# A recommender's attention kernel: the bias of the attended history goes through the first layer once, and the end of the program is put in another order

## The reference

```python
cand = candidate_features @ Wi + bi                  # 512 x 64
hist = history_features @ Wi + bi                    # 512 x 200 x 64
hidden = relu((cand @ Wq)[:, None, :] + hist @ Wk)
scores = where(mask, hidden @ Wv, -1e9)
attn = softmax(scores, axis=1)
interest = einsum('bs,bse->be', attn, hist)
avg = sum(hist * mask, axis=1) / lens
x = concatenate([interest, cand, avg], axis=1)       # 512 x 192
x = relu(bn(x @ W1 + b1)); x = relu(bn(x @ W2 + b2)); x = relu(bn(x @ W3 + b3))
return sigmoid(x @ Wo + bo)[:, 0]
```

## Time and profile before

| what | us |
|---|---|
| median of three runs | 212.09 (210.8 to 212.43) |
| the profiled execution's own time | 211.71 |
| its span, first to last instruction | 209.7 |
| PE busy in the span | 200.9 |
| DVE busy in the span | 176.8 |
| ACT busy in the span | 103.5 |
| POOL busy in the span | 62.6 |

### The profile page before, as it was taken

How to read it: one execution, slowest core, us unless ns; L and a number is a source line. 1 busy time by engine, 2 the same in 40 slices (tenths; PEclk the granted TensorE clock), 3 DMA queues, 4 the chain that set the end, 5 groups by cost and what they waited for, 6 DMA issues and landing times.

```text
span 209.7 us, 6308 instructions
## 1 busy us (share of the span) xinstructions
PE 200.9 (96%) x2126; PEld 83.6 (40%) x2126; DVE 176.8 (84%) x1086; ACT 103.5 (49%) x302; POOL 62.6 (30%) x112
## 2 busy tenths in 40 slices
PE   7999999999999999999999999999999999997793
PEld 3422434343434434343434343343444343433422
DVE  1458578989989898989899898989898998998890
ACT  2145355545465553555453655535554536556523
POOL 7903330606051321406060513224060605131000
PEclk9999999999999999999999999999999999999985
DMA  6999999797979797987969797978879793000000
GB/s 201 398 426 416 412 419 391 245 328 249 323 245 322 237 320 266 309 307 269 321 242 300 268 323 237 316 262 317 303 253 326 238 318 130 0 0 5 3 0 0
DMA packets 10225, 53.72 MB, mean 256 GB/s; under 512 B 1105, under 2 KB 2001, under 8 KB 10194
## 3 DMA queue, kind: packets, MB, share of 16 engines
q1 hardware_dynamic: 9906, 52.95, 70.7%
q10 hardware_dynamic: 288, 0.37, 0.6%
HBM read 53.32 MB, written 0.00 MB: 254 GB/s over the span
## 4 chain that ended last, share of the span: by engine, by line
PE 87%; DVE 8%; ACT 2%; issue 2%; DVEq 0%; ACTq 0%
PE hist_ps L396 42%; PE key_ps L411 24%; PE score_ps L422 10%; PE attn_ps L441 5%; DVE scratch L552 3%; DVE kept L539 3%; PE score_ps L366 2%; PE score_ps L473 1%; PE score_ps L465 1%; ACT hidden L306 1%; ACT x L326 1%; PE score_ps L468 0%; PE hist_ps L411 0%; ACT result L334 0%; DVE attended L552 0%
## 5 line engine op out<-in xcount | busy, mean ns | idle before, releaser
L306 ACT ACTIVATE hidden<-key_ps,query 128x200 f32<-128x200 f32 x252 | 86.8, 427 | 54.3 <-PE key_ps L411 54.3
L396 PE MATMUL hist_ps<-history,params 128*64 128x400 f32 x512 | 100.3, 512 | 0.0
L539 DVE SCALAR_TENSOR_TENSOR kept<-item,lens,hist_ps 128x200 f32<-128x200 f32 x256 | 92.7, 419 | 7.2 <-PE hist_ps L396 7.2
L552 DVE CUSTOM_DVE_ANT_0 scratch<-attn_ps,kept 128x200 f32<-128x200 f32 x240 | 73.3, 363 | 9.2 <-PE attn_ps L441 9.2
L411 PE MATMUL key_ps<-kept,params 64*64 64x400 f32 x504 | 57.0, 521 | 0.9 <-ACT hidden L306 0.4
L396 PEld LDWEIGHTS hist_ps<-history,params 128*64 128x64 f32 x512 | 31.2, 136 | 37.1 <-issue 28.4
L259 POOL TENSOR_SCALAR attn<-weights,inv_sum 128x200 f32<-128x200 f32 x15 | 6.5, 435 | 112.6 <-DVE inv_sum L567 112.6
L411 PEld LDWEIGHTS key_ps<-kept,params 64*64 64x64 f32 x504 | 13.6, 131 | 35.9 <-issue 26.7
L422 PE MATMUL score_ps<-hidden,wv_rows 128*32 128x200 f32 x512 | 25.3, 336 | 1.2 <-ACT hidden L306 1.2
L441 PEld LDWEIGHTS attn_ps<-parts,spread 64*64 64x64 bf16 x480 | 15.7, 107 | 24.5 <-issue 19.0
L314 ACT ACTIVATE weights<-scores,neg_max 128x200 f32<-128x200 f32 x16 | 7.4, 462 | 35.5 <-DVE neg_max L561 35.5
(11 more groups left out here) (69 smaller groups left out, 59.0 us busy)
## 6 DMA issues: line engine op xcount, KB each, us to landing
history<-history_dram SPq DMA_DIRECT2D x63, 800.0 KB, 5.0
history<-history_dram SPq DMA_DIRECT2D x2, 400.0 KB, 4.7
candT<-candidates_dram SPq DMA_DIRECT2D x1, 256.0 KB, 5.5
params<-parameters_dram SPq DMA_DIRECT2D x1, 248.5 KB, 12.1
params<-parameters_dram ACTq DMA_DIRECT2D x1, 226.5 KB, 2.4
lens_raw<-lengths_dram ACTq DMA_DIRECT2D x1, 136.0 KB, 3.8
probability<-result SPq DMA_DIRECT2D x1, 2.0 KB
```

The source lines that it names most:

```text
L306: act.activation(hidden[:, g % HID_SLOTS, v, :], banks[:, v, at * SEQ:(at + 1) * SEQ], ACT.Relu, bias=query[:, 2 * g + v:2 * g + v + 1]).t ...
L396: product = pe.matmul(hist_ps[64 * h:64 * h + 64, g % 2, 0:QCOLS], param("wi"), history[:, slot, h, 2 * at:2 * at + 2, :].rearrange("f p s ...
L539: dve.scalar_tensor_tensor(out=kept[:, g % KEPT_SLOTS, u, :], in0=item[:, :], scalar=pair_len[:, col:col + 1], in1=hist_ps[:, g % 2, u * S ...
L552: dve.tensor_tensor_reduce(scratch[:, at, v, :], banks[:, at, v * SEQ:(v + 1) * SEQ], kept[:, q % KEPT_SLOTS, v, :], 1.0, 0.0, ALU.mult, A ...
```

## The change

The addition of bi to the attended sums goes: a matmul of one column puts bi through the first layer's weights once, ACT copies the result to `fold_bias`, POOL adds it to the first layer's shift, and stage 1 of the network reads `attended`. PE does that matmul in unit 5, behind the projections; ACT the copy behind `relu(5)`; POOL waits for the copy within its batch norm chain. Fewer matmuls on zeros are issued: 4 for 6, 2 for 4, 2 for 6. The network's parts become 228 and 28 pairs, so that `mean(0)` comes one unit earlier in the loop (unit 59). At the end `mean(1)` stands before the attended sums of unit 57, the fourth sum of unit 59 stands behind the first instruction of the last split, ACT does stage 1 of part 0 before it loads the sigmoid's table, and PE and ACT do stages 2 to 4 of part 0 earlier.

```diff
+FOLD_AT = 5
-MORE_WARMUPS = 6
-GAP_WARMUPS = 4
-TAIL_WARMUPS = 6
+MORE_WARMUPS = 4
+GAP_WARMUPS = 2
+TAIL_WARMUPS = 2
-PART_UNITS = UNITS - 6
+PART_UNITS = FREE_AT
...
@@ gpsimd
             pool.wait_ge(bn_steps, 3)
+
+            pool.wait_ge(fold_ready, 1)
+            pool.tensor_tensor(bn_shift[:, 0:1], bn_shift[:, 0:1], fold_bias[:, :], ALU.add).then_inc(bn_steps, 1)
             pool.tensor_tensor(bn_scale[:, :], bn_scale[:, :], bn_power[:, :], ALU.pow).then_inc(bn_steps, 1)
-            pool.wait_ge(bn_steps, 4)
+            pool.wait_ge(bn_steps, 5)
...
@@ scalar, the loop over units and the end
                 relu(unit)
+                if unit == FOLD_AT:
+                    act.wait_ge(fold_product, 1)
+                    act.activation(fold_bias[:, :], attn_ps[:, 1, 0:1], ACT.Copy).then_inc(fold_ready, 1)
             exponent(LAST)
+            mlp_stage(0, 1)
             act.activation(table_loader[:, :], param("bo", slice(0, 1)), ACT.Sigmoid)
-            for stage in range(1, 4):
-                mlp_stage(0, stage)
+            mlp_stage(0, 2)
+            mlp_stage(0, 3)
+            mlp_stage(0, 4)
             mlp_stage(1, 1)
             mlp_stage(1, 2)
-            mlp_stage(0, 4)
             mlp_stage(1, 3)
             mlp_stage(1, 4)
@@ tensor
                 if stage == 1:
-                    pe.wait_ge(interest_ready, n + 1)
+                    pe.wait_ge(attn_summed, pairs.stop)
...
-                        product = pe.matmul(z1[:, h, pairs], w1[rows, 0, :], interest[rows, pairs],
+                        product = pe.matmul(z1[:, h, pairs], w1[rows, 0, :], attended[rows, pairs],
...
+                if unit == FOLD_AT:
+                    pe.wait_ge(late_landed, 16)
+                    pe.wait_ge(bias_ready, 1)
+                    pe.matmul(attn_ps[:, 1, 0:1], w1[0:EMB, 0, :], param("bi", slice(0, EMB)),
+                              start=True, stop=True).then_inc(fold_product, 1)
...
                         pe.wait_ge(query_ready, 1)
+                        pe.wait_ge(fold_ready, 1)
                     spread_attn(unit - DELAY)
...
             for _ in range(TAIL_WARMUPS):
                 keep_busy((LAST + 1) % 2)
+            mlp_stage(0, 2)
             spread_attn(first + 3)
             spread_attn(first + 4)
-            mlp_stage(0, 2)
+            mlp_stage(0, 3)
             spread_attn(first + 5)
-            mlp_stage(0, 3)
             spread_attn(first + 6)
+            mlp_stage(0, 4)
             mlp_stage(1, 0)
-            mlp_stage(0, 4)
@@ vector
-            def store_interest(n):
...
             first = UNITS - DELAY
+            mean(1)
             attended_sum(first)
-            store_interest(0)
-            mean(1)
             attended_sum(first + 1)
             maximum(LAST)
-            attended_sum(first + 2)
+            attended_sum(first + 2, (0, 1, 2))
             invert(LAST)
...
             dve.tensor_scalar(part_a[:, :], weights[:, bank, :], inverse, param("keep1"),
                               ALU.mult, ALU.mult).then_inc(split_steps, 1)
+            attended_sum(first + 2, (3,))
...
             for unit in range(first + 3, UNITS):
                 attended_sum(unit)
-            store_interest(1)
```

More of the change, by code:

```diff
@@ L110, in build @@
         attended = sb("attended", [128, HALF])
-        interest = sb("interest", [128, HALF])
+        fold_bias = sb("fold_bias", [128, 1])
         average = sb("average", [128, HALF])
@@ L180, in build @@
         average_ready = sem("average_ready")
-        interest_ready = sem("interest_ready")
+        fold_product = sem("fold_product")
+        fold_ready = sem("fold_ready")
         z1_ready = sem("z1_ready")
@@ L282, in _ @@
             pool.wait_ge(bn_steps, 3)
+            pool.wait_ge(fold_ready, 1)
+            pool.tensor_tensor(bn_shift[:, 0:1], bn_shift[:, 0:1], fold_bias[:, :], ALU.add).then_inc(bn_steps, 1)
             pool.tensor_tensor(bn_scale[:, :], bn_scale[:, :], bn_power[:, :], ALU.pow).then_inc(bn_steps, 1)
-            pool.wait_ge(bn_steps, 4)
+            pool.wait_ge(bn_steps, 5)
             pool.tensor_tensor(bn_scale[:, :], bn_scale[:, :], param("g"), ALU.mult).then_inc(bn_steps, 1)
-            pool.wait_ge(bn_steps, 5)
+            pool.wait_ge(bn_steps, 6)
             pool.tensor_tensor(bn_shift[:, :], bn_shift[:, :], bn_scale[:, :], ALU.mult).then_inc(bn_steps, 1)
-            pool.wait_ge(bn_steps, 6)
+            pool.wait_ge(bn_steps, 7)
             pool.tensor_tensor(bn_shift[:, :], bn_shift[:, :], param("be"), ALU.add).then_inc(bn_ready, 1)
```

## The result

The changed kernel took 217.53 us (median of six runs, 217.31 to 218.06), the kernel before 211.75 (six runs, 210.8 to 214.19): a ratio of 1.0274, 95% interval 1.0251 to 1.0297, so 5.8 us slower. The profiled execution of the changed kernel took 217.36, its span 215.3. The forecast was 216.3 within 213.9 to 218.2: the sign, the place and the mechanism were right, and the sum missed 1.4 us of the span (5.6 for 4.25).

The account below looks back on a forecast made before the run. PE was taken to bound the loop, busy 60.00 of 60 us. POOL's wait +4.1, start -0.25, end -1.2 gave +2.65, with the clock's 1.6 +4.25: 216.3 us on the median of 212.09, range 213.9 to 218.2.

Parts of the forecast that it names:

- the start: Before the loop's steady pace: fewer matmuls on zeros, less the fold's matmul, gain 0.25 us, bounds 0 and 0.5.
- the clock: Behind PE's pause in unit 7: TensorE's clock falls to half pace, costing 1.6 us, from a span of 1.4 to 2.9.
- POOL's wait: POOL's batch norm chain waits for ACT's copy, delaying the first split and PE's first spread: 4.1 us, bounds 3.7 and 4.4.
- the loop's end: `mean(0)` in unit 59 instead of 60: same work meets same slack, 0 us, bounds -0.36 and +0.56.
- The rival in which the pause is made good: In the loop behind the pause PE catches up 4.1 us, so only start and end count: 210.6 us; chance 0.05.
- The rival in which it holds: Behind the pause in unit 7 the clock stays full, leaving +2.65 us: 214.7 us; chance 0.32.
- The 0.195 per matmul: At the start, each matmul on zeros dropped saves 0.195 us; four save 0.78.
- the landing of unit 1: At the start, unit 1's load lands at 9.52, so PE starts about 9.6 and keeps 0.4 of the 0.78 us.
- The fold's matmul: In unit 5 on PE, the one-column matmul costs 0.15 us, between nothing and 0.26.
- Behind the loop: After the loop: DVE's dropped addition and reordered sums, and PE's earlier stages, gain 1.2 us, bounds 0.2 and 1.9.
- The low end of the stated range: Whole kernel at 213.9 us: the clock holds and the end gains 1.9 rather than 1.2.

Follow-up runs that it names:

- experiment 1: Changed kernel with POOL's whole batch norm chain, including its wait for the fold, moved behind the first split: 210.76 us, 0.9959 of the kernel before.
- experiment 2: Kernel before plus only one wait in POOL's batch norm chain, for the ReLUs of unit 5: 217.70 us, 1.0290 of before.
- experiment 4: Changed kernel with ACT's copy of the fold's column ahead of the ReLUs of unit 5: 212.61 us, 1.0062 of the kernel before.
- experiment 5: Changed kernel, copy ahead of unit 5's ReLUs but held until their keys are there: 213.16, 213.33, 215.47 and 215.76 us, ratio 1.0129 to before.
- Experiment 3: Changed kernel plus 20 matmuls on zeros on PE in unit 7, ahead of the first spread: 215.07 us, 1.0163 of the kernel before.
- experiment 7: Experiment 1's kernel with stage 0 of part 1 earlier on PE: 210.73 us; or with PE's and ACT's old stage order, six matmuls on zeros: 210.61 us.
- the five series: Kernels with POOL's chain behind the first split: experiment 1, its rerun, that with the old start's matmuls on zeros, experiment 7's two: 210.76, 210.99, 210.98, 210.73, 210.61 us.

## Why the prediction was right, and where its sum was short

The 1.4 us that the sum missed are four terms, all in the same direction: 0.55 of the start, 0.4 of the clock, 0.3 of POOL's wait and 0.1 of the loop's end.

- **POOL's wait** was forecast from the earlier trace rows at 4.1 us, less 0.25 of the start. PE idled 4.01. Beyond the 0.31 of the start the spread begins 4.2 later (33.00 - 28.47 - 0.31; before, it had overlapped the keys by 0.2), and with the spread at the lower clock (0.55 for 0.38) the loop stands 4.4 later. The wait is shown as the cause from both sides, by experiments 1 and 2. That none is earned back in the loop held too: the lag is +6.70 at unit 9 (37.98 - 31.28 by PE's timeline before, where that projection stood at 31.28) and +6.79 at unit 61. The rival in which the pause is made good falls.
- **The clock** was forecast to fall, at 1.6 us. It fell, and from 33.48 to 37.98 one unit took 4.50 us and not 2.50: 2.0 us. The rival in which it holds is what 8 of 10 and 2 of 4 runs with the shorter pauses of experiments 4 and 5 show; at this length it fell, six of six by their clocks. The reasoning held that some of the slow time passes within the pause: of 6.8 us at the lower level (30.9 to 37.7) 2.1 did. The size was short because the whole stretch was longer than the 2.85 to 5.7 us that the start suggested.
  The Trainium skill's page "TensorE: Matmul & The Clock Gate" says that activity releases the throttle and its section on HAM oscillation shows waits between bursts bringing it back. Experiment 3, which fills the pause with matmuls and keeps 1.56 us and a granted clock of 1.00, agrees.
- **The start** is the step that failed: 0.25 gained was the forecast, 0.3 lost was measured (keys of unit 6 at 28.09 for 27.78), 0.16 of it up to unit 1. The 0.195 per matmul was taken from a stretch at the full clock, and a part of the executions isn't at it yet by the first projection; the trace of before showed it, with 1.49 for six of them from 4.51 on, 0.25 each. And the 0.4 that the landing of unit 1 was to leave of the gain was reckoned from the 10.00 of the chain of waits, where the timeline has 9.83; from there it is 0.2. How much is lost here is in part the luck of one profile: in experiment 1's unit 1 starts at 9.71. The fold's matmul cost what was put down, 0.14: from the projection of unit 5 to the first score PE took 1.80 us (21.60 - 19.80) for 1.66 (21.30 - 19.64).
- **The loop's end**: `mean(0)` a unit earlier makes a wait of 0.50 and removes one of 0.36; 0.1 lost for 0.
- **Behind the loop**: 1.2 forecast, 1.2 measured (6.79 - 5.58), but for partly other reasons, so that the agreement is in part luck. The maximum gains 0.77 (0.66 forecast), `rest` another 0.12 (0.13), the first of the 16 sums gives 0.09 back, since the spread now stands behind stage 2 on PE, and PE was 0.15 late for stage 1 of part 1, because stages 4 and 0 ran there at the lower clock (0.05 late forecast). So 0.4 of the gain lies between the last sum and stage 1 (0.55 before, 0.15 now), for 0.5 forecast. The order of the stages, to which I gave the room for this, isn't needed where six matmuls on zeros stand ahead of it (experiment 7).

The sum with measured terms: +4.4 + 2.0 + 0.3 + 0.1 - 1.2 = +5.6, the difference of the spans (215.3 - 209.7). The low end of the stated range comes out at 214.0 from its terms (212.09 + 4.1 - 0.25 - 1.9), not 213.9; nothing hangs on it.

**The better version.** With POOL's chain behind the first split the change is worth 0.3 to 0.6%; the lowest of the five series of such kernels is experiment 7's, 210.61 us, 6.9 us under the changed kernel. The intervals of the five overlap.

## What to carry to other kernels

A wait that is put into an engine's list holds up everything behind it in that list, also what has nothing to do with it: ask what is next on that engine, when it is due, and put late, small work behind it. Here a scale and shift that ACT first needs at 197.79 us, in the network, was made from 18 on, ahead of a split due at 28. And price a stop of a busy TensorE with its clock: 4 us of idle time cost 6. Where a kernel's runs fall into two groups, list the runs with their clocks before reading the median.

## What the runs showed of the hardware that I had not expected

- In a busy loop the clock fell in all runs with a pause of 4.01 or 3.80 us (10 of 10; one of each kernel profiled, the others by their times), and by the times and clocks in 2 of 4 at 2.68. Ahead of the fall PE had been idle for 1.9 us in one profile and for 2.9 in the other. Two of ten runs with a pause of 1.53 us look the same, but so do 4 of 60 of the kernel before, which has no such pause. One fall costs 2.0 to 2.5 us, beside the pause.
- At the start, the moment of the clock's rise moves between executions of one kernel, so that four equal matmuls take 0.85 or 1.52 us. Matmuls on zeros ahead of the work can't be tuned by one profile. The granted clock in the windows doesn't show this: it is 1.00 from the first microsecond in all profiles here; only the durations do.
